# First loads in halves and a reordered first batch in a gated cross-attention kernel with experts

## What is computed

```python
x = x + jnp.tanh(g_xattn[0]) * xattn(_layernorm(x), ctx, W_kv, W_q, W_proj, b_proj)
x = x + jnp.tanh(g_ffn[0]) * ffn(_layernorm(x), gate_w, w_up, w_down, sg_gate, sg_up, sg_down)
# xattn: 16 heads of 16 features
k, v = split(ctx @ W_kv); q = x @ W_q
out = softmax(q k^T * 16**-0.5) v @ W_proj + b_proj
# ffn: the 2 best of 8 experts (softmax of their logits as weights), plus a shared one
expert(x) = silu(x @ wg.T) * (x @ wu.T) @ w_down.T
```

## Time and profile before

| | us |
|---|---|
| three runs | 499.70, 499.72, 500.06 (median 499.72) |
| the profiled execution, its own time | 499.88 |
| its span, first to last instruction | 497.7 |
| TensorE busy | 477.6 |
| VectorE busy | 306.7 |
| ScalarE busy | 259.8 |
| GpSimd busy | 183.9 |
| mean granted clock of TensorE | 0.994 |

### The profile page before, as it was taken

One profiled execution on the slowest core, in us unless ns is written; L12 is line 12 of the kernel. 1 busy time (PEld: TensorE's weight loads), 2 busy tenths in 40 slices (PEclk: granted clock), 3 DMA queues, 4 the chain that ended last, 5 costly groups with the idle time before them and its releaser, 6 DMA issues.

```text
span 497.7 us, 7742 instructions
## 1 busy us (share of the span) xinstructions
PE 477.6 (96%) x2783; PEld 285.8 (57%) x2783; DVE 306.7 (62%) x574; ACT 259.8 (52%) x415; POOL 183.9 (37%) x216
## 2 busy tenths in 40 slices
PE   8999999999999999999989898999999999999992
PEld 7665433333333233235445355589899799799992
DVE  3766779999999998995574799232333333333331
ACT  1665277777777777776544202105445346244430
POOL 4800187773311111111000060503556747667333
PEclk9999999999999999999999999999999999999997
DMA  7632408867742555210022001413334435435232
GB/s 244 233 105 101 133 21 225 241 161 196 207 134 66 160 159 161 73 57 24 32 85 86 2 1 42 128 42 75 64 45 68 70 55 78 72 55 84 33 33 32
DMA packets 36741, 48.30 MB, mean 97 GB/s; under 512 B 6240, under 2 KB 29920, under 8 KB 36704
## 3 DMA queue, kind: packets, MB, share of 16 engines
q1 hardware_dynamic: 21536, 26.16, 18.6%
q0 software_dynamic: 7344, 9.84, 12.9%
q10 hardware_dynamic: 7824, 11.81, 7.3%
HBM read 30.16 MB, written 14.29 MB: 89 GB/s over the span
## 4 chain that ended last, share of the span: by engine, by line
PE 88%; DVE 9%; ACT 1%; issue 1%; POOLq 0%; POOL 0%
PE ps L1283 68%; PE ps L1369 13%; PE ps L1642 2%; PE ps L1653 2%; PE ps L1289 1%; DVE unit_region L1169 1%; PE ps L1675 1%; DVE rows L893 1%; DVE neg_max L928 1%; DVE unit_region L1063 1%; DVE ctx_region L1178 1%; ACT ctx_region L763 1%; PE ps L1299 1%; DVE unit_region L1095 0%; PE ps L1361 0%
## 5 line engine op out<-in xcount | busy, mean ns | idle before, releaser
L763 ACT ACTIVATE ctx_region<-ps 128x512 f32<-128x512 f32 x256 | 140.7, 594 | 46.9 <-PE ps L1283 46.9
L928 DVE TENSOR_REDUCE neg_max<-ps 128x2 f32<-128x1024 f32 x128 | 150.9, 1209 | 21.3 <-PE ps L1283 19.2
L1283 PE MATMUL ps<-unit_region 96*128 96x512 bf16 (+1 forms) x512 | 128.3, 380 | 0.9 <-ACT ctx_region L763 0.7
L1283 PEld LDWEIGHTS ps<-unit_region 96*128 96x128 bf16 (+1 forms) x512 | 45.0, 97 | 100.8 <-ACT ctx_region L763 45.2
L1283 PE MATMUL ps<-unit_region,ctx_region 128*128 128x128 f32 (+1 forms) x824 | 97.6, 274 | 1.4 <-DVE x_sb L1070 1.4
L1283 PEld LDWEIGHTS ps<-unit_region,ctx_region 128*128 128x128 f32 (+1 forms) x824 | 94.2, 188 | 2.5 <-DVE x_sb L1070 2.2
L655 POOL DMA_INDIRECT out<-unit_region x39 | 61.2, 1570 | 54.1 <-DMA out<-unit_region 30.9
L1283 PE MATMUL ps<-dn_region,unit_region 128*128 (+1 forms) x294 | 70.0, 381 | 0.0
L1240 DVE TENSOR_TENSOR unit_region<-unit_region,ps 128x384 f32<-128x384 f32 x35 | 19.4, 554 | 71.1 <-ACT unit_region L860 64.7
L843 ACT COPY ctx_region<-up_region 128x1536 f32 x33 | 48.5, 1472 | 27.3 <-PE ps L1283 27.2
L1283 PEld LDWEIGHTS ps<-dn_region,unit_region 128*128 128x128 f32 x294 | 53.2, 190 | 9.2 <-issue 2.8
(11 more groups left out here) (200 smaller groups left out, 463.6 us busy)
## 6 DMA issues: line engine op xcount, KB each, us to landing
up_region<-in_w_upT ACTq DMA_DIRECT2D x9, 768.0 KB, 4.5
qk_parts<-up_region SPq DMA_DIRECT2D x24, 192.0 KB, 3.1
unit_region<-qk_parts SPq DMA_DIRECT2D x24, 192.0 KB, 4.2
dn_region<-in_w_downT ACTq DMA_DIRECT2D x9, 384.0 KB, 5.2
unit_region<-up_region SPq DMA_DIRECT2D x48, 64.0 KB, 2.6
unit_region<-qk_parts SPq DMA_DIRECT2D x24, 128.0 KB, 4.3
ctx_region<-in_ctxT SPq DMA_DIRECT2D x4, 512.0 KB, 10.8
x_rows<-rows SPq DMA_DIRECT2D x4, 512.0 KB, 3.9
```

What stands on the lines that cost most here:

```text
L763: nc.scalar.activation(probs[:, k % 8, :], bank(SCORE_HOME[u, k]), ACT.Exp).then_inc(exp_done, 1)
L928: nc.vector.tensor_reduce(neg_max[:, s, 2 * p:2 * p + 2], bank(2 * (p % 2), 2), AX.X, ALU.max, negate=True).then_inc(max_done, 1)
L1283: return nc.tensor.matmul(o_, w, m, start=start, stop=stop)
```

## The change

The load of the key weights and that of the first context are cut into the two halves of the contraction, each with a semaphore of its own; the weights' halves move to the head of ScalarE's queue, ahead of x. The first key projection runs the first half of the contraction for both output halves and then the second. In batch 0 all value products come ahead of the turn of x; batch 1 keeps its order. Bias, output weights and the expert gate's weights go from ScalarE's queue to the end of SP's first loads, with the wait for the zeroed gate tile. Nine products of a tile that VectorE has set to zero take the place of the 36 transpositions.

```diff
-WARM = 36
+WARM = 9
...
+        warm = dn_region[:, 0:P]
...
-            w_kv_rows = w_kv.rearrange("(c p) n -> p c n", p=P)
-            sp.dma_start(wkv_sb[:, :, 0:D], w_kv_rows[:, :, 0:D]).then_inc(wk_in, 16)
-            load_ctx(0)
-            sp.dma_start(wkv_sb[:, :, D:2 * D], w_kv_rows[:, :, D:2 * D]).then_inc(wv_in, 16)
+            for c in range(DC):
+                sp.dma_start(ctx_sb[:, c, 0:T], ctxT[c * P:(c + 1) * P, 0:T]).then_inc(first_ctx_in[c], 16)
+            sp.dma_start(wkv_sb[:, :, D:2 * D], w_kv.rearrange("(c p) n -> p c n", p=P)[:, :, D:2 * D]).then_inc(wv_in, 16)
             for b in range(1, B):
                 load_ctx(b)
                 sp.dma_start(x_sb[:, b * TB:(b + 1) * TB, :], x_dram[:, b * TB:(b + 1) * TB, :]).then_inc(x_in[b], 16)
+            sp.dma_start(bias_sb[:, :], b_proj.partition_broadcast(P)).then_inc(small_in, 16)
+            sp.dma_start(wp_sb[:, :, :], w_proj.rearrange("(c p) n -> p c n", p=P)).then_inc(small_in, 16)
+            sp.wait_ge(gate_zero, 1)
+            sp.dma_start(gate_sb[:, :, 0:E], gateT.rearrange("(c p) n -> p c n", p=P)).then_inc(small_in, 16)
...
         @block.scalar
         def _(act):
+            for c in range(DC):
+                act.dma_start(wkv_sb[:, c, 0:D], w_kv[c * P:(c + 1) * P, 0:D]).then_inc(wk_in[c], 16)
             act.dma_start(x_sb[:, 0:TB, :], x_dram[:, 0:TB, :]).then_inc(x_in[0], 16)
...
-            act.dma_start(bias_sb[:, :], b_proj.partition_broadcast(P)).then_inc(small_in, 16)
-            act.dma_start(wp_sb[:, :, :], w_proj.rearrange("(c p) n -> p c n", p=P)).then_inc(small_in, 16)
-            act.wait_ge(gate_zero, 1)
-            act.dma_start(gate_sb[:, :, 0:E], gateT.rearrange("(c p) n -> p c n", p=P)).then_inc(small_in, 16)
...
         def _(dve):
+            nc.vector.memset(warm[:, :], 0.0).then_inc(warm_set, 1)
             nc.vector.memset(gate_sb[:, :, :], 0.0).then_inc(gate_zero, 1)
...
+            pe.wait_ge(warm_set, 1)
+            for i in range(WARM):
+                mm(bank(7)[:, 0:P], warm[:, :], warm[:, :])
             pe.wait_ge(ident_done, 1)
-
-            for i in range(WARM):
-                nc.tensor.transpose(bank(7)[:, 0:P], ident[:, :], ident[:, :])
...
+            def project_first_k():
+                for d in range(DC):
+                    pe.wait_ge(wk_in[d], 16)
+                    pe.wait_ge(first_ctx_in[d], 16)
+                    for c in range(DC):
+                        last = mm(bank(K_BANK + c), wkv_sb[:, d, c * P:(c + 1) * P], ctx_sb[:, d, 0:T], d == 0, d == DC - 1)
+                last.then_inc(k_ps, 1)
+
...
+            project_first_k()
+            project_v(0, (0, 1))
+            project_v(0, (2, 3))
+            turn_xn(0)
+            project_q(0, 0)
+            project_q(0, 1)
+            project_k(1, 0)
...
```

More of the change, by code:

```diff
@@ L322, in build @@
         ctx_in = [sem(f"ctx_in{b}") for b in range(B)]
-        wk_in, wv_in, wq_in = sem("wk_in"), sem("wv_in"), sem("wq_in")
+        first_ctx_in = [sem(f"first_ctx_in{c}") for c in range(DC)]
+        wk_in = [sem(f"wk_in{c}") for c in range(DC)]
+        wv_in, wq_in, warm_set = sem("wv_in"), sem("wq_in"), sem("warm_set")
         gates_in = sem("gates_in")
@@ L1316, in project_q @@
                     last.then_inc(q_ps, 1)
+            def project_first_k():
[5 more added lines that the diff above has]
+                last.then_inc(k_ps, 1)
             def project_k(b, c):
                 if c == 0:
-                    if b == 0:
-                        pe.wait_ge(wk_in, 16)
                     pe.wait_ge(ctx_in[b], 16)
@@ L1410, in slot @@
                     also(k)
-            for b in range(2):
-                project_k(b, 0)
-                project_k(b, 1)
-                project_v(b, (0, 1))
-                turn_xn(b)
-                project_v(b, (2, 3))
-                project_q(b, 0)
-                project_q(b, 1)
+            project_first_k()
[5 more added lines that the diff above has]
+            project_k(1, 0)
+            project_k(1, 1)
+            project_v(1, (0, 1))
+            turn_xn(1)
+            project_v(1, (2, 3))
+            project_q(1, 0)
+            project_q(1, 1)
             def first_pair(w, p):
```

## The result

The changed kernel takes 503.46 us, median of five executions (501.2, 502.13, 503.46, 503.47, 504.27), against 499.70 for the kernel before in the same comparison: 1.0064 times as long, 95% interval 1.0038 to 1.009. It is slower. The profiled execution is the fastest of the five, 501.2 us with a span of 499.4.

What follows compares the result with a forecast made beforehand. TensorE, busy 96% of the span and 88% of the chain, was taken as the bound. 3.3 us from warm-ups and loads, less 0.7 for the clock and 1.3 for the hole, gave 1.3 off 499.72: 498.5 us, range 497.6 to 499.5.

Steps and rivals of the forecast that it cites:

- the lead of 1.3: First query projection starts 1.3 us earlier: 3.3 from warm-ups and loads, less 0.7 for lower clock and 1.3 for hole.
- Warm-ups: TensorE's start: nine zeroed-tile products run from 1.05 to 4.95 us, ending 3.3 us earlier than the 36 transpositions.
- Key loads: First halves of key weights and context land by 4.95 us, second ones by 6.2 us, so nothing is waited for.
- x: First x batch on ScalarE's queue lands by 8.2 us at the latest, rows at 11.0 to 12.0, before the turn at 12.55.
- rival 3: First x batch lands late, near 9.5 us, as queues share by packets; lead 0.55 us, 499.2 us; chance 13%.
- The hole of the copy: Before batch 0's query products, ScalarE's copy of the turned x is no longer covered: a new hole of 1.3 us.
- The clock: TensorE's clock rises at 6.4 us, inside the first key projection, which costs 0.72 us at the lower level.
- rival 2: Clock stays low through the first key projection, taking 6.9 us; query starts at 17.4 us, 501.2 us in all; chance 4%.
- SP's copies, small weights, later stages: SP's 48 copies start near 17 us, gaining 0.4 to 0.8; slack covers that and three added loads; later stages keep the lead.
- the mark: First record of the first query projection on TensorE, 16.00 us before, forecast at 14.7 us.
- rival 4: The lead is absorbed by SP's copies or something chained to them: 499.7 us; chance 10%.
- Rival 1: Clock rises earlier, at the end of the warm-ups: lead of 1.9 us at query, 497.8 us; chance 15%.

Runs made afterwards that it cites:

- the one that alternates: Changed kernel with the key weights' halves back on SP's queue, each ahead of its context half, x heading ScalarE's queue: 503.56 us, ratio 1.0076.
- the filled kernel: Changed kernel with 16 unused transpositions of the identity ahead of the turn of x and 8 behind it: 502.17 us, ratio 1.0046.
- weights moved only: Kernel before with only the uncut key weights moved from SP's queue to the head of ScalarE's: 501.96 us, ratio 1.0044.
- moved, early start: Kernel before with uncut key weights at the head of ScalarE's queue and 12 zeroed-tile products replacing the 36 transpositions: 500.2 us, ratio 1.0016.

## Why the prediction was wrong

The forecast was 498.5 us in a range of 497.6 to 499.5 (499.72 less the lead of 1.3 is 498.4, a slip of 0.1); measured were 503.46. By its own steps:

- *Warm-ups*: right. 1.11 to 4.93 us, forecast 1.05 to 4.95.
- *Key loads*: nearly. The first halves landed at 5.0 (context) and 5.5 us (weights) for 4.95, the second at 7.0 and 7.1 for 6.2, just ahead of their products; the key projection started at 5.55 us instead of 4.95; the clock came up sooner than 6.4 us, near 4.4 us by the warm-ups' durations, and no key record lasted over 667 ns, and values began at 9.06 us, forecast 9.1.
- *x*: **the step that failed.** I wrote that x "completes 768 KB of it, where the query weights did: 8.2 us at the latest". It landed at 11.2 us, rows at 15.0 instead of 11.0 to 12.0, the turn at 15.02 instead of 12.55. Depth in a queue took the place of a look at what the other queue held. The query weights' 8.2 us came with key weights in rows of 1 KB at the head of SP's queue; after the change rows of 2 KB stood there. The equal bytes of 4 to 6 us that I held against rival 3 were a mean of two unlike microseconds. The queues' packets, MB and share of 16 engines' time before, from 4 to 5, 5 to 6 and 6 to 7 us:

```profile
q10 hardware_dynamic: 325, 0.32, 90.5%
q1 hardware_dynamic: 42, 0.07, 19.8%
...
q1 hardware_dynamic: 141, 0.29, 80.2%
q10 hardware_dynamic: 64, 0.06, 18.3%
...
q1 hardware_dynamic: 143, 0.22, 59.3%
q10 hardware_dynamic: 143, 0.15, 43.4%
```

  and of the changed kernel from 8 to 9 us, with x (q10) under way beside the contexts (q1):

```profile
q1 hardware_dynamic: 129, 0.25, 65.9%
q10 hardware_dynamic: 135, 0.13, 38.4%
```

  In 6 to 7 us before it was packet for packet, 143 to 143, and so it nearly was in 8 to 9 us of the changed kernel, 129 to 135, where ScalarE's queue, with rows of half the size, moved half the bytes. The Trainium skill, "DMA: Bandwidth & Descriptors", section "Queues, rings and completion order", says that an engine takes its queues by turns, a packet each; these microseconds agree, the two from 4 to 6 us do not, nor does 6 to 7 us of the changed kernel, with 227 packets of ScalarE's queue to 144. And the depth in bytes did not tell the landing. Before, ScalarE's queue had moved its 768 KB (0.79 MB) when the query weights landed at 8.2 us. In the changed kernel it had moved 0.80 MB by 9.0 us, only 0.8 us later; but when x landed, at 11.2 us, it had moved 1.04 MB, nearly all of the query weights behind x too. The last piece of x came 2.2 us after the queue's first 768 KB. Why, no run shows.
- *The hole of the copy*: right, 1.19 us for 1.3. But behind a late turn it is added to the wait for x. Turn to query was 2.29 us, forecast 2.17.
- *The clock*: a term that was missing. I priced it at its rise only, and wrote against rival 2 that nothing interrupts TensorE before the hole. Behind the wait of some 2 us and that hole it fell, by times and mean clocks in 11 of 16 executions, for 2.9 us in the one that has a trace.
- *SP's copies, small weights, later stages*: the copies began at 19.39 instead of 17 us, as the copied turn came late, and did no harm; SP's loads were issued by 13.5 us, forecast 13; the small weights were free; and the mark's lateness arrived at the end undiminished, which also answers rival 4.

**The rivals.** Rival 3 had the wait right and the size wrong: 768 KB at 9.5 us and 499.2 us; x landed at 11.2 us and the time without the fall of the clock was 501.2. ScalarE's queue did get a third of the bytes up to 6 us (0.29 of 0.93 MB), and its 768 KB were through by 9.0 us; what rival 3 had wrong is the step from these bytes to the landing of x. With 11.2 us in its own rule, 0.1 us of loss for each 0.1 us behind 8.8, the lead of 1.3 turns into a loss of 1.1 us, near the 1.3 measured. The sign named in the prediction, a wait of the turn for VectorE's rows, is in the profile. The whole start is thinner now, too. Totals from 0 to 6 us, before and changed:

```profile
DMA packets 1011, 1.18 MB, mean 196 GB/s; under 512 B 32, under 2 KB 839, under 8 KB 1011
```

```profile
DMA packets 716, 0.93 MB, mean 155 GB/s; under 512 B 60, under 2 KB 464, under 8 KB 716
```

These totals go with which load heads SP's queue: 1.17 to 1.33 MB in the five other profiles with all key weights there and the context behind, 0.84 to 1.03 MB in the ten others with the context there; the one that alternates has 1.07. It is a correlation over 18 profiles, in which a context at the head always means key weights on another queue. Why, no run shows, and it stays open. Rival 2, the lower level through the key products, did happen, in the profile of the filled kernel in part, with a granted clock of 1.00 beside records of 1061 ns; in the changed kernel the wait for x would cover it, though no run shows that. Rival 1's early rise did happen too, and was worth nothing, since keys and values were no longer on the path.

The 503.5 us are thus: 499.7, plus 1.3 at the query mark for the late x with the copy's hole behind it (in all three profiles), plus 2.5 that are left for the fall of the clock (2.9 in its trace). Parts alone cost: moving the key weights 2.2 us (its profile has a fall of the clock in it), the order of the values 2.0, cutting 0.8, small weights and warm-ups nothing. They don't add up to the whole; that the late x and the order share one wait is the likely reason, which was not tried by itself.

## What to carry to other kernels

At this kernel's start the loads competed, and moving one load earlier made another late. At such a start list what each engine waits for first, and read the shares of queues microsecond by microsecond, in packets as well as bytes. The bytes ahead of a load in its queue are not its landing. A start pulled ahead of its next input gained nothing at the end, and the gap that opened in TensorE cost the clock behind it in most executions. Price every new wait of some microseconds twice, at both levels of the clock.

## What the runs showed of the hardware

- Two queues side by side took turns by packets in some microseconds: 137 of 0.25 MB against 139 of 0.14 MB, again, in the kernel with the moved weights from 8 to 9 us. In others they did not (325 to 42, 227 to 144).
- Loads issued one behind the other on one queue do not land at a steady pace: the two weight halves of 128 KB were there at 5.5 and 7.1 us, and 768 KB cut in four landed 1.2 us later than in two (8.8 us for 7.6). The last piece of x came 2.2 us after its queue had moved as many bytes as stood up to its end.
- A load on GpSimd's queue at the program's start took 8.1 us for 256 KB, against 3.9 us for the same bytes at the head of SP's, beside other loads in both.
- The moment of the clock's rise differs between executions: near 4.4 us in the first profile of the changed kernel, near 9.8 us in that of the filled one, with the same instructions up to there. The granted clock of the profile says 1.00 in both; there only the records' durations (421 ns for 128 columns, 1061 for 512) tell.
- The clock fell to 0.50 behind gaps of only 1.95 and 1.19 us, 0.9 us apart, and stayed up behind 2.35 and 1.19 us in another execution of the same kernel. A single gap of 2.02 us (weights moved only) was followed by 0.50, one of 1.61 us (moved, early start) was not.
